# Dispatching the first token group between the last memory tiles of a memory-and-experts layer

## The reference, cut to what matters

```
z = x @ W_in; z_mem = causal depthwise convolution, 4 taps
p_w  = exp(clip(scale * s, -20, 20) + log_tw)        # weight of a token, 32 heads
num  = cumsum(p_w * (cos, sin)(k_val * theta))       # 1024 + 1024 columns a token
y    = silu(sum over 8 phases of num * query / cumsum(p_w))
x1   = layernorm(x + y @ W_out)
probs = softmax(x1 @ router.T); the best 2 of 8 experts, weights normalised
out  = sum over the 2 of w_e * relu(x1 @ up_e.T)**2 @ down_e.T
     + relu(x1 @ up_shared.T)**2 @ down_shared.T
result = layernorm(x1 + out)
```

## Time and profile before

| | us |
|---|---|
| median of 3 runs | 535.51 |
| lowest, highest | 534.37, 537.81 |
| profiled execution | 533.17 |
| its span in the trace | 531.3 |

### The profile page before, as it was taken

The page is one execution under the profiler, slowest core; times in us unless marked ns, Lnnn a source line. Parts: engine busy times, 40 slices in busy tenths (PEclk is TensorE's granted clock), DMA queues, the critical chain, the costliest instruction groups (busy, mean ns, idle before and its releaser), DMA issues.

```text
span 531.3 us, 7487 instructions
## 1 busy us (share of the span) xinstructions
PE 440.9 (83%) x2153; PEld 288.9 (54%) x2153; DVE 376.9 (71%) x839; ACT 355.7 (67%) x534; POOL 310.1 (58%) x261
## 2 busy tenths in 40 slices
PE   5758899998999988856879999959999999999100
PEld 1213344433343433323657877749999999999100
DVE  7497999998999999999756566282333334554296
ACT  1848799998999999922355655617666676666244
POOL 3251567777677777761277877732555554655440
PEclk9987999999999999979689999979999999999655
DMA  7010010109866654000011111122222221221463
GB/s 258 0 40 0 2 41 1 43 15 388 313 234 226 226 209 162 1 1 1 6 48 50 47 46 51 52 70 66 67 80 68 74 63 54 68 61 46 148 227 99
DMA packets 39448, 48.55 MB, mean 91 GB/s; under 512 B 5408, under 2 KB 25058, under 8 KB 38896
## 3 DMA queue, kind: packets, MB, share of 16 engines
q1 hardware_dynamic: 34048, 39.06, 21.7%
q0 software_dynamic: 5216, 8.70, 5.3%
q10 hardware_dynamic: 144, 0.31, 0.2%
HBM read 19.17 MB, written 29.11 MB: 91 GB/s over the span
## 4 chain that ended last, share of the span: by engine, by line
PE 36%; DVE 33%; issue 12%; POOL 9%; ACT 7%; DMA 3%; SPq 0%; ACTq 0%; DVEq 0%; POOLq 0%
PE routed_ph L1312 12%; PE routed_po L1325 12%; DVE memory_prod L690 10%; DVE memory_y_raw L699 9%; POOL table_scratch L1017 5%; DVE memory_feat L678 4%; PE dispatch_sph L877 3%; PE dispatch_spo L887 3%; POOL memory_feat L451 2%; PE routed_px L1300 2%; DVE memory_query L673 1%; PE memory_nsum L556 1%; ACT memory_feat L356 1%; DVE finish_xo L1528 1%; ACT memory_feat L360 1%
## 5 line engine op out<-in xcount | busy, mean ns | idle before, releaser
L451 POOL TENSOR_TENSOR memory_feat<-memory_feat,memory_p_tok 128x1024 f32<-128x1024 f32 x64 | 121.6, 1923 | 57.8 <-ACT memory_feat L365 57.7
L556 PE MATMUL memory_nsum<-memory_feat,tri 128*128 128x512 f32 x256 | 118.7, 607 | 15.1 <-DVE memory_prod L690 7.3
L1288 POOL DMA_INDIRECT pick_scratch<-routed_ob,routed_xg x71 | 71.5, 1007 | 73.0 <-DVE routed_ob L1409 57.8
L556 PEld LDWEIGHTS memory_nsum<-memory_feat,tri 128*128 128x128 f32 x256 | 48.1, 194 | 76.5 <-issue 72.5
L690 DVE TENSOR_TENSOR memory_prod<-memory_nsum,memory_query 128x1024 f32<-128x1024 f32 x64 | 75.4, 1217 | 2.8 <-PE memory_nsum L556 2.7
L1017 POOL DMA_INDIRECT table_scratch<-dispatch_xrow,dispatch_slot x64 | 63.1, 986 | 18.9 <-issue 18.0
L699 DVE TENSOR_REDUCE memory_y_raw<-memory_prod 128x128 f32<-128x2048 f32 x32 | 73.1, 2285 | 1.0
L1358 ACT ACTIVATE routed_rel<-routed_ph 128x512 f32<-128x512 f32 x71 | 42.3, 597 | 45.9 <-PE routed_ph L1312 45.9
L1312 PE MATMUL routed_ph<-routed_xs,routed_w1c 128*128 128x256 f32 (+1 forms) x368 | 72.3, 340 | 0.0
L1409 DVE TENSOR_SCALAR routed_ob<-routed_po,routed_xg 128x128 f32<-128x128 f32 x71 | 22.6, 348 | 69.7 <-PE routed_po L1325 69.7
L1325 PE MATMUL routed_po<-routed_w2c,routed_hid 128*128 128x128 f32 x568 | 71.1, 275 | 0.5 <-ACT routed_hid L1367 0.5
(11 more groups left out here) (177 smaller groups left out, 623.8 us busy)
## 6 DMA issues: line engine op xcount, KB each, us to landing
table_scratch<-memory_blank SPq DMA_DIRECT2D x68, 260.0 KB, 2.9
finish_pick<-pick_scratch SPq DMA_DIRECT2D x16, 256.0 KB, 5.4
routed_xg<-table_scratch SPq DMA_DIRECT2D x25, 130.0 KB, 2.2
x_tok<-x SPq DMA_DIRECT2D x4, 512.0 KB, 3.8
w<-w_up SPq DMA_DIRECT2D x2, 1024.0 KB, 9.1
w<-w_down SPq DMA_DIRECT2D x2, 1024.0 KB, 11.1
out<-finish_xo SPq DMA_DIRECT2D x8, 256.0 KB, 2.3
routed_xg<-table_scratch SPq DMA_DIRECT2D x21, 65.0 KB, 1.9
```

What stands on the lines that cost most here:

```text
L451: last = nc.gpsimd.tensor_tensor(v, v, pv, ALU.mult)
L556: last = nc.tensor.matmul(nsum[:, o:o + 512], tri[:], feat[:, i % U, h, q * 512:(q + 1) * 512], start=True, stop=True)
L1288: nc.gpsimd.indirect_dma_start(out=pick_dram, in_=ob[:, u, h, :], in_offset=None, out_offset=bass.IndirectOffsetOnAxis(ap=xg[:, t % XU, h, ...
```

## The change

- Dispatch of group 0 goes between tiles 28 and 31. VectorE: constants and residual 0 after tile 28, normalise 0 after tile 29, residual 1 and choose 0 after tile 30; place 0, weigh 0, count 0, normalise 1 after tile 31. TensorE: turn and projection 0 after tile 28, turn 1 after 29, turn x, projection 1 and routing 0 after 30, rank 0 after 31. ScalarE has a tail too: silu of groups 0 and 1 after the cosines at tiles 12 and 20, y copy 0 at 28, silus 2 to 5, two constants and y copy 1 at 29. GpSimd: root 0 after the multiplies and carry of tile 30, root 1 after those of tile 31.
- The reductions of tiles 28 to 31 and the last two inversions run in the dispatch's loop on VectorE; the products of tiles 29 to 31 go to free buffers of `feat`. The last two scales run on GpSimd behind scatters 1 and 3.
- Roots of groups 0, 1, 2, 4 and 6 stay with GpSimd; those of 3, 5 and 7 are made on VectorE from a shifted bit pattern and four Newton rounds.
- The rank's operands are float32r (one pass a matmul); the constants of it are made by ScalarE.
- The shared expert's adds come one group later, and the loops of TensorE and ScalarE are reordered.
- Finish: TensorE sums the two picks with the identity into PSUM, eight banks; ScalarE normalises all four tiles; four buffers in place of two.

```diff
@@ build
         def _(act):
-            mem.scalar(act)
-            dis.scalar(act)
+            tail, rest = dis.scalar(act)
+            mem.scalar(act, tail)
+            rest()
@@
-            mem.gpsimd(pool, tail)
-            rest()
+            scale = mem.gpsimd(pool, tail)
+            rest(scale)
@@ memory
-        INVERT = {4: 0, 8: 1, 12: 2, 16: 3, 20: 4, 24: 5, 28: 6, 30: 7}
+        INVERT = {4: 0, 8: 1, 12: 2, 16: 3, 20: 4, 24: 5}
@@
-                if i % B == 3 and i > B:
+                if i % B == 3 and B < i < NT - 1:
                     scale(i // B - 1)
-            tail(NT)
-            scale(TPB - 1)
+            return scale
@@
-                if b % 2 == 1 and i + 1 < NT:
+                if b % 2 == 1 and i + 3 < NT:
                     queries((i + 1) // 2)
                 sums(i)
+                if i == NT - 4:
+                    queries(NT // 2 - 1)
@@
+            def products(i):
+                return prod if i <= NT - B else feat[:, (i - 1) % U]
@@
-                if i + 1 == NT:
-                    tail(i)
-                reduce(i)
+                if i < NT - B:
+                    reduce(i)
...
+                if i == NT - 4:
+                    q_part(NT // 2 - 1)
+                tail(i)
+            return reduce, invert
@@ dispatch, tensor
             def tail(i):
-                if i == NT - 2:
+                if i == NT - 4:
                     turn_y(0)
+                    project(0)
+                elif i == NT - 3:
                     turn_y(1)
-                    project(0)
+                elif i == NT - 2:
+                    turn_x(0)
+                    project(1)
+                    route(0)
+                elif i == NT - 1:
+                    pe.wait_ge(ones_set, 1)
+                    rank(0)
@@ dispatch, tensor, the loop after
+                for g in range(1, NG):
+                    if g + 1 < NG:
+                        turn_x(g + 1)
                     if g + 2 < NG:
-                        turn_y(g + 2)
+                        project(g + 2)
                     up(g, 0)
                     if g + 1 < NG:
-                        turn_x(g + 1)
-                    if g:
-                        down(g - 1, 0)
+                        route(g + 1)
+                    down(g - 1, 0)
                     up(g, 1)
+                    down(g - 1, 1)
                     if g + 1 < NG:
                         rank(g + 1)
...
@@ dispatch, scalar
+            def tail(i):
+                if i in (12, 20):
+                    silu(i // 8 - 1)
+                if i == NT - 4:
+                    keep_y(0)
+                if i == NT - 3:
+                    for g in range(2, NG - 2):
+                        silu(g)
+                    nc.scalar.copy(tri_r[:], tri[:])
+                    nc.scalar.activation(ones_r[:], tri[:], ACT.Copy, bias=1.0, scale=0.0).then_inc(ones_set, 1)
+                    keep_y(1)
@@ dispatch, gpsimd
-                        if n == g * GT + 2 and r == 1 and g + 2 < NG:
+                        if n == g * GT + 2 and r == 1 and g + 2 in POWERS:
                             inverse_root(g + 2)
@@
             def tail(i):
-                if i == NT - 1:
-                    inverse_root(0)
-                if i == NT:
-                    inverse_root(1)
+                if i >= NT - 2:
+                    inverse_root(i - (NT - 2))
-            def rest():
+            def rest(scale):
                 for g in range(NG):
                     scatter(g)
+                    if g in (1, 3):
+                        scale(TPB - 2 + g // 2)
@@ dispatch, vector, normalise
-                link(nc.vector.scalar_tensor_tensor(rstd[:], newton[:, 1], 1.5, root[:], ALU.add, ALU.mult))
+                if g in POWERS:
+                    dve.wait_ge(root_done, POWERS.index(g) + 1)
+                else:
+                    link(nc.vector.tensor_scalar(bits[:], var[:].bitcast(I32), 1, None, ALU.logical_shift_right))
+                    link(nc.vector.tensor_scalar(root[:].bitcast(I32), bits[:], -1.0, float(ROOT_SEED), ALU.mult, ALU.add))
+                for n in range(1 if g in POWERS else 4):
...
@@ dispatch, vector, tail and rest
                 if i == NT - 4:
                     constants()
-                if i == NT - 2:
                     residual(0)
-                if i == NT - 1:
+                elif i == NT - 3:
                     normalise(0)
+                elif i == NT - 2:
                     residual(1)
                     choose(0)
-                    normalise(1)
-                    place(0)
-                    weigh(0)
-                    count(0)
-
-            def rest():
+            def rest(reduce, invert):
+                place(0)
+                weigh(0)
+                count(0)
+                normalise(1)
+                reduce(NT - 4)
                 for g in range(NG):
+                    if g >= 2:
+                        add_shared(g - 2)
...
+                    if g < 3:
+                        reduce(NT - 3 + g)
+                    if g in (0, 2):
+                        invert(TPB - 2 + g // 2)
@@ finish
-        def gpsimd(pool):
+        def tensor(pe):
             for g in range(NG):
-                pool.wait_ge(picked[g], 32)
-                if g >= 2:
-                    pool.wait_ge(res_done, g - 1)
-                nc.gpsimd.tensor_tensor(both[:, g % 2], pick[:, 0, g * GT:(g + 1) * GT, :],
-                                        pick[:, 1, g * GT:(g + 1) * GT, :], ALU.add).then_inc(both_done, 1)
+                pe.wait_ge(picked[g], 32)
+                for r in range(2):
+                    last = nc.tensor.matmul(both[g][:], ident[:],
+                                            pick[:, r, g * GT:(g + 1) * GT, :].rearrange("p t d -> p (t d)"),
+                                            start=(r == 0), stop=(r == 1))
+                last.then_inc(both_done, 1)
@@
-                for t in range(GT - 1):
+                for t in range(GT):
                     last = nc.scalar.activation(xo[:, s, t, :], res[:, s, t, :], ACT.Identity,
@@
-                t = GT - 1
-                nc.vector.tensor_scalar(xo[:, s, t, :], res[:, s, t, :], mv[:, s, t, 0:1], rstd[:, s, t:t + 1],
-                                        ALU.subtract, ALU.mult).then_inc(xo_part, 1)
```

217 lines of the change are left out of this document (109 added, 108 removed).

## The result

| | before | after |
|---|---|---|
| median, us | 535.28 (4 runs) | 518.11 (4 runs) |
| lowest, highest | 534.37, 537.81 | 516.82, 518.77 |
| profiled execution, span | 533.17, 531.3 | 518.65, 516.8 |

The ratio of the times is 0.9664, with a 95% interval of 0.9635 to 0.9692 (the two medians by themselves give 0.968). The forecast was 524.0, the range 516 to 531; the measured time is inside it, but outside the 520 to 528 that the forecast's own account allowed, at the place of the first rival. The forecast had three stretches (start, queue, rest); here is the whole span cut by the same marks.

The account below looks back on a forecast made before the run. Ahead of the routed stage, GpSimd's back-to-back scatters were taken as the bound, behind a late first scatter. Start -13.3, silu +0.8, queue +1.3, finish -0.3 gave -11.5: from the median 535.51 to 524.0 us, range 516 to 531.

Parts of the forecast that it names:

- the first rival: Whole kernel: no port loss in the transition, queue never waits, TensorE's clock holds; 518 us, chance 0.15.
- no scatter waiting above 1 us: Scatter queue, a sign: scatter waits total at most 1 us for each of groups 1, 2 and 4.
- (a): Memory loop's tail: first scatter starts earlier with group 0 between tiles 28 and 31; -13.3 us, bounds -17 to -8.
- The 1.0 for a half clock: Way to the first scatter: 1.0 us added for TensorE's pauses and sums 31 perhaps at half clock.
- (b): Memory loop: silu of groups 0 and 1 on nearly full ScalarE costs 0.4 us each, +0.8.
- (c): Scatter queue: three roots leave -2.9, two scales enter +2.4, waits +1.8; sum +1.3 us.
- waits of 0.4 + 0.6 + 0.4: Scatter queue: waits for late slots of groups, by VectorE's work count; taken as 1.8 us with handoffs.
- TensorE's saving hidden: Dispatch stage: TensorE's earlier start and five-pass rank stay hidden behind GpSimd's longer queue, 11.1 to 11.3 us a group.
- (d): Finish: period 2.63 for 3.27, -2.7; fourth ScalarE op +0.4; slower first sum +2.0; net -0.3 us, bounds -2.5 to +5.
- Half clock in the transition: Way to first scatter, a rival: sums 31 at half clock, normalise waits longer; -8 for -13.3, 529 us, chance 0.14.
- half clock throughout the finish: Finish, a rival: TensorE stays at half clock, +5 for -0.3; 529 us, chance 0.09.
- the handoffs in series: Dispatch, a rival: each group a round trip; mild form about 532 us, chance 0.05; full form, 545 at p=15, 0.05.

Follow-up runs that it names:

- e5: Kernel before with VectorE's constants after tile 30 instead of tile 28: 533.45 us, ratio 0.9946.
- e6: Changed kernel with the reductions of tiles 28 to 31 back in the memory loop: 524.93 us, ratio 0.9791.
- e9: Changed kernel as it is, run again in another set: 517.58 us, ratio 0.9662.
- e1: Kernel before with only the new finish, on a chip where the kernel before took 554.73 us: 550.23 us, ratio 0.9874.
- e10: Changed kernel with all roots but the last (seven) on GpSimd: 518.34 us, ratio 0.9665.
- e8: Changed kernel with the rank's float32r operands back to fp32, ten records in place of five: 520.72 us, ratio 0.971.
- e11: Changed kernel with the table of tiles cut in two and group 6's shared addition between the halves: 518.49 us, ratio 0.9674.
- e12: Changed kernel with the table of tiles cut in two and seven roots on GpSimd: 517.16 us, ratio 0.965.
- e7: Changed kernel with root 0 behind GpSimd's multiplies of tile 31, ahead of its carry: 521.09 us, ratio 0.9716.
- e2: Changed kernel with the old finish, on a chip where the kernel before took 554.73 us: 551.1 us, ratio 0.9959.

## Why the prediction was right, and where it was off

The time fell inside the range, and nearly all of the gain came where it was forecast, in the way to the first scatter. But 518 was not the account with the best chance. Of its signs, the first scatter, the five roots, the 2.7 us stall of normalise 0 and the first sum of 3.5 came true; "no scatter waiting above 1 us" and the period of 2.6 did not.

**(a) The start, -13.3 forecast.** Right in mechanism and order, too small by 2.6 in size. Without the loop's part, the stretch from tile 28 to the first scatter went from 40.2 to 24.25, by 15.9; e5 shows 4.5 of it for the constants and e6 5.2 for the reductions, and if the two add, the rest, 6.2, is the group's place two tiles earlier, which was not tried alone. Four terms were mis-sized. The 1.0 for a half clock was not needed (1.00 granted over the stretch, with waits of 1.78 and 1.38). The constants stalled for 1.89 and ended near 230.7, which is 228.8 on the clock of before, where I had put 229.9. And with them all that follows came a microsecond earlier: the multiplies of tile 31 began at 232.2 on that clock (I had 233.3) and took 3.77. The fourth goes the other way and hides part of this: I had the first scatter 0.2 us behind the slots, and it came 1.1 behind them (248.44 to 249.53). The forecast stall of normalise, to the end of both multiplies, is there as forecast: 0.88 and 1.83 us for ops of 0.16.
For these small ops rule and row had made different forecasts, and the ops are held up. The Trainium skill, "SBUF — State Buffer", section "Who interferes with whom", has a VectorE op with two SBUF inputs wait out a GpSimd op that reads; this trace agrees, with the 0.88 and 1.83.

**(b) Silu in the loop, +0.8 forecast.** +0.67 at tile 28 by one pair of traces (224.07 in e9 against 223.40), +1.88 by another. A term of this size can't be read from single executions: kernels without silu in the loop reach tile 28 at 223.40, 224.08 and 225.16 (before, e1, e5), and those with it, on the undisturbed chips, at 223.38 to 226.34 (e6, e10). Of the +1.88, 1.6 arise at tile 13, where e9, with the same program, does not have them. No run here shows the term by itself.

**(c) The queue, +1.3 forecast, +2.1 measured.** Three roots went out and two scales came in, at about the forecast prices. The step that failed is "waits of 0.4 + 0.6 + 0.4": group 1 waits not at all, groups 2 and 4 wait 2.08 and 2.59 us. I had counted VectorE's new work by sum, and not that its four normalise ops would stand beside the scale that I had myself moved into the queue; they took 1.5 and 1.4 us more than those of group 4. Removing the Newton rounds, which make these ops late, removed both waits (e10); removing the reductions did not (e6). By the waits alone (4.1 us above the usual gaps, for the 1.8 that I took) the term would have missed by more. It was helped by something that the sum put at nothing: the 64 scatters took 61.8 us in all where they had taken 63.1 (966 ns each for 986). No run explains that.
The step that called TensorE's saving hidden failed in the other direction, and is the finding of this case. The rank's single pass is worth 2.6 us (e8), because TensorE, through the list of tiles, became the last to end the stage. That the stage still ended only 0.7 us later than the scatters allow is why the forecast did not suffer.

**(d) The finish, -0.3 forecast, -2.8 measured.** The first sum was right (3.5 us). The period was not: I added 0.42 for ScalarE's fourth op, less 0.15, to a period of 2.36, and it came to 2.28. I had added it to a period that ScalarE did not set. By the rows shown under the result, VectorE set the 3.27 and the 2.36 of before, and ScalarE waited 1.15 us a group for the statistics (0.19 where GpSimd was silent). With its normalise op gone VectorE needs less than 2.28, and waits 0.12 us of each group for ScalarE's root (498.21 to 498.33); the ring through ScalarE's four ops is the longer now, by that little. So the fourth op is in the 2.28, but the 2.36 that I added it to had gone. This is read from the traces, not tried by itself. 7 x (2.63 - 2.28) = 2.45 us. The -2.8 lies just outside the bounds of this term, -2.5 to +5. The clock did neither what the lower bound assumes (full) nor the upper (half throughout): it was 0.58 over the first sum (490.1 to 493.6), 1.00 from there to 505.5, and VectorE never waits for TensorE again.

**The sum** was -11.5; the spans differ by 14.5, and by 15.6 with e9. The rest to the 17.2 of the medians is that the profiled execution of before lay 2.1 us under its median, and that of after 0.5 above its own. Of the rivals, the first (518, "all meshes") gave the number, but by another way, and that is luck: it asked that normalise is not held up and that the queue never waits, but normalise was held up for 2.7 us and the queue waited for 4.1. Only its clock held. What made up for the rest was mainly a finish 2.5 us better than forecast. Half clock in the transition, half clock throughout the finish and the handoffs in series did not occur.

## What to carry to other kernels

When a queue is moved forward by much, list every chain that ends in the same place, with its slack, before calling its savings hidden: here the one that ended 5 us ahead of the rows became the last. Before adding an op to an engine, see from the chain whether that engine sets the pace. Count not only how much work an engine gets but what runs beside it: a small VectorE op next to a long GpSimd pair cost up to the rest of that pair here, so an op in front of the pair that holds GpSimd back can be the better order. And a shorter chain to an idle TensorE may only move the same idle time to another place, with the same low clock behind it (e5, e11, e12).

## What the runs showed of the hardware

- A VectorE op on four columns is held up beside GpSimd's multiplies too: 2.83 us for 0.17 (e7), 0.88 and 1.83 for 0.16 (after). What happens between the two multiplies of a pair is not one rule. In the trace of after a waiting TENSOR_TENSOR got through there (L1115 ended at 236.03, halfway through the pair from 234.10 to 237.87), and the next op waited for the second. In e7 a waiting TENSOR_SCALAR did not get through: it stood from 233.25 to 236.08, the end of the pair from 232.01 to 236.05. Which of the two happens, and why, was not tried.
- TensorE after pauses of the same size is not always at the same clock: in the memory loop the sums of tile 13 run after 2.23 us of wait at a granted clock of 0.78 (window 125 to 130) in the trace of after, and after 2.14 us at 1.00 in that of e9, with the same program. This makes 1.6 us between executions. Of the eight traces of this loop from undisturbed chips, two have the 0.78 (after and e8):

```profile
125.00:130.00 5.00, 2.77 (x7) 1.34 (x6) 3.66 (x3) 4.98 (x6) 3.44 (x3) 0.78 1.01 421
```

```profile
125.00:130.00 5.00, 2.86 (x9) 1.30 (x8) 3.76 (x4) 4.97 (x6) 3.24 (x3) 1.00 1.02 423
```

- In the finish of e1, after 7.12 us of idleness, TensorE's weight loads stand 0.85 us apart in the first sums (granted clock 0.53 from 522 to 526) and 0.43 from 526.02 on (1.00 from 526 to 530). The Trainium skill, "TensorE: Matmul & The Clock Gate", section "What's actually happening", has activity release the throttled default; the trace agrees.
- One of the chips took longer over the dispatch stage with each of the four kernels that ran on it: from the first scatter to the first one of the routed stage it is 120.5 us in e1 (101.9 in the kernel before), and 128.5 in e2 (104.2 in the changed one). The way to the first scatter and the finish did not differ by more than 1 us. The cause was not tried.
